# A relative-position attention layer on one core: one bias term computed on the queries' rows and moved by transfers, in place of PE transposes

## The reference

```python
q, k, v = (shape_heads(x @ W + b) for W, b in ...)      # 16 batches, 16 heads, 256 tokens, 8 features
scores = einsum('bhsd,bhkd->bhsk', q, k) / sqrt(24)
c2p = einsum('bhsd,hkd->bhsk', q, pos_k)                # 64 buckets
c2p = take_along_axis(c2p, idx(s - k))                  # -> [s, k], value depends on bucket(s - k)
p2c = take_along_axis(einsum('bhsd,hkd->bhsk', k, pos_q), idx(k - s)).swapaxes(-1, -2)
probs = softmax(scores + (c2p + p2c) / 4)
ctx = einsum('bhsk,bhkd->bhsd', probs, v)
```

## Time and profile before

| | |
|---|---|
| median of 3 runs | 1324.26 us (1322.44 to 1327.71) |
| the profiled execution, its own time | 1330.51 us |
| its span in the trace | 1328.7 us |
| mean granted TensorE clock | 0.886 of full speed |
| busy: PE, DVE, ACT, POOL | 1048.3, 863.0, 727.5, 460.4 us |

### The profile page before, as it was taken

How to read it: one execution, slowest core, us unless ns; L and a number is a source line. 1 busy time by engine, 2 the same in 40 slices (tenths; PEclk the granted TensorE clock), 3 DMA queues, 4 the chain that set the end, 5 groups by cost and what they waited for, 6 DMA issues and landing times. The chain is left out here.

```text
span 1328.7 us, 34742 instructions
## 1 busy us (share of the span) xinstructions
PE 1048.3 (79%) x9380; PEld 834.1 (63%) x9380; DVE 863.0 (65%) x2997; ACT 727.5 (55%) x1755; POOL 460.4 (35%) x506
## 2 busy tenths in 40 slices
PE   4793515787353899999999999999999998734886
PEld 3793513777232677777777777777777776624776
DVE  6886754555570677777777777777677775652554
ACT  2236411344282677777777777777677774212443
POOL 2503213765200433333333333333333332005764
PEclk9897556999585899999999999999999998656999
DMA  5920052331263222221212222221312220033431
GB/s 136 227 52 0 0 180 92 111 103 54 72 254 120 64 59 62 59 68 50 69 50 69 56 63 67 59 69 50 69 50 69 55 55 1 1 147 97 114 96 42
DMA packets 83508, 103.23 MB, mean 78 GB/s; under 512 B 16473, under 2 KB 71200, under 8 KB 82944
## 3 DMA queue, kind: packets, MB, share of 16 engines
q1 hardware_dynamic: 77824, 89.92, 25.1%
q0 software_dynamic: 5632, 12.70, 2.8%
HBM read 67.86 MB, written 35.74 MB: 78 GB/s over the span
## 5 line engine op out<-in xcount | busy, mean ns | idle before, releaser
L1230 POOL TENSOR_SCALAR ds_scores<-ds_scores,ds_max 128x256 f32<-128x256 f32 x256 | 236.3, 923 | 434.3 <-DVE ds_max L1468 434.2
L1460 DVE TENSOR_TENSOR ds_p2c<-ds_bank,ds_p2c 128x512 f32<-128x512 f32 x256 | 176.4, 689 | 147.9 <-PE ds_bank L1289 113.4
L1468 DVE CUSTOM_DVE_ANT_0 ds_scores<-ds_bank,ds_p2c 128x256 f32<-128x256 f32 x512 | 197.2, 423 | 0.2 <-DVE ds_p2c L1460 0.2
L1289 PE MATMUL ds_bank<-all_constants,ds_c2p_t 128*128 128x128 f32 x1024 | 165.4, 284 | 0.0
L1407 ACT ACTIVATE all_xt<-ds_bank 128x512 f32<-128x512 f32 x256 | 152.6, 596 | 21.4 <-PE ds_bank L1307 8.9
L1307 PE MATMUL ds_bank<-all_constants,ds_scores 128*128 128x128 f32 x1024 | 154.6, 273 | 2.4 <-ACT all_xt L1407 1.6
L1289 PEld LDWEIGHTS ds_bank<-all_constants,ds_c2p_t 128*128 128x128 f32 x1024 | 111.3, 141 | 31.9 <-issue 20.7
L1307 PEld LDWEIGHTS ds_bank<-all_constants,ds_scores 128*128 128x128 f32 x1024 | 120.2, 140 | 7.6 <-issue 2.0
L1390 ACT ACTIVATE ds_c2p_t<-ds_bank 128x256 f32<-128x256 f32 x256 | 77.6, 390 | 56.7 <-PE ds_bank L1280 56.7
L1383 ACT ACTIVATE ds_p2c<-ds_bank 64x512 f32<-64x512 f32 x128 | 75.7, 591 | 54.7 <-PE ds_bank L1261 31.6
L1280 PE MATMUL ds_bank<-d_qr,ds_tab 64*128 64x128 f32 x1024 | 77.3, 292 | 33.1 <-DMA ds_tab<-scratch_tables 27.8
(11 more groups left out here) (285 smaller groups left out, 2011.8 us busy)
## 6 DMA issues: line engine op xcount, KB each, us to landing
ds_tab<-scratch_tables SPq DMA_DIRECT2D x64, 248.0 KB, 3.5
slots_in<-all_zero SPq DMA_DIRECT2D x2, 5180.0 KB, 37.9
ds_qs<-scratch_q_parts SPq DMA_DIRECT2D x32, 288.0 KB
ds_ks<-scratch_k_parts SPq DMA_DIRECT2D x96, 96.0 KB
d_qr<-scratch_qk SPq DMA_DIRECT2D x512, 4.0 KB
d_kr<-scratch_qk SPq DMA_DIRECT2D x512, 4.0 KB
0fe_xb<-slots_in SPq DMA_DIRECT2D x40, 129.5 KB, 2.1
1fe_xb<-slots_in SPq DMA_DIRECT2D x40, 129.5 KB, 2.1
```

The source lines that it names most:

```text
L1230: pool.tensor_scalar(S[b % NS][:, 1, :], S[b % NS][:, 1, :], mx[:, 2 * b + 1:2 * b + 2], None, ALU.subtract).then_inc(s_sub1, 1)
L1289: last = pe.transpose(pt1[b % 2][:, st * SEQ + kt * P:st * SEQ + (kt + 1) * P], CT[half][:, kt, b, st * P:(st + 1) * P], con["ident"])
L1460: dve.tensor_tensor(z, pt1[b % 2][:, :].rearrange("p (a k) -> p a k", a=2), z, ALU.add).then_inc(s_z, 1)
L1468: last = dve.tensor_tensor_reduce(out=S[b % NS][:, st, :], in0=pqk[b % 2][:, st * SEQ:(st + 1) * SEQ], in1=PC[half][:, st, b, :], scale=1. ...
```

## The change

The c2p term is made the other way round. The sparse query rows are the stationary operand and the table moves, so the term comes out with (token group, batch) on partitions and keys along the row. Four matmuls of 64 rows by 64 columns are laid side by side, for two groups of tokens at once. This is one fill "c2p", of which a unit has four (`CROSS`): 8 matmuls with 256 moving columns, into two PSUM banks `pc[0]` and `pc[1]` (those that held the results of `t1`). ACT copies each bank (128x512) into one of four slots of a new tile `STAGE`. From there transfers (`spread`) bring it to the queries' rows of `CT`, which is now laid (query, batch, half, key). For each of the four fills there are three transfers: 64 partitions of 2 KB to 8 partitions of 16 KB, twice, and 128 partitions of 2 KB to 16 partitions of 16 KB. The transposes `t1` go away, and DVE adds `CT` from SBUF. The scores are written back into `PC` rather than into `S`. The "far", "edge", "near" and "pair" fills of c2p go away, and with them the table `far_e`. The two row tiles become one tile `QKR`, filled by 16 transfers of 8 KB rather than 32 of 4 KB. Such a transfer stands on SP's queue in groups of four between the spreads. DVE waits at the start of each unit for all twelve spreads of that unit.

```diff
@@ attend
-        ENDS = [m.sb(f"ends{i}", [9 * DB, 2, 2 * FAR], BF16) for i in range(2)]
-        CT = [m.sb(f"c2p_t{i}", [P, 2, HALF, SEQ]) for i in range(2)]
+        ENDS = [m.sb(f"ends{i}", [9 * DB, 2 * FAR], BF16) for i in range(2)]
+        CT = [m.sb(f"c2p{i}", [P, HALF, 2, SEQ]) for i in range(2)]
+        STAGE = m.sb("stage", [P, 4, 2 * SEQ])
-        S = [m.sb(f"scores{i}", [P, 2, SEQ]) for i in range(NS)]
-        pb, pt1, pqk, pt2, pav = bank[0:2], bank[2:4], bank[4:6], bank[6], bank[7]
+        pb, pc, pqk, pt2, pav = bank[0:2], bank[2:4], bank[4:6], bank[6], bank[7]
+        CROSS = [("c2p", 0, i) for i in range(NB16 // 4)]
-        FILLS = [PAIRS[0][0], PAIRS[0][1], PAIRS[1][0], FARS[0][0], EDGE[0], FARS[0][1], NEAR[0],
-                 PAIRS[1][1], FARS[1][0], NEAR[1], FARS[1][1], EDGE[1]]
+        FILLS = [CROSS[0], CROSS[1], NEAR, CROSS[2], FARS[0], PAIRS[0], CROSS[3], PAIRS[1], FARS[1], EDGE]
-        SHARE = [1, 1, 1, 2, 2, 1, 2, 2]
+        SHARE = [1, 1, 1, 1, 2, 1, 2, 1]
@@ SP
+            def load_rows(head, half, first, count):
+                for s in range(first, first + count):
+                    at = slice(s * P, (s + 1) * P)
+                    sp.dma_start(QKR[half][(15 - s) * DB:(16 - s) * DB, :, at],
+                                 dram["qk"][:, bass.ds(head * DB, DB), half * HT + at.start:half * HT + at.stop].rearrange("j p n -> p j n")).then_inc(s_rows[half], 16)
+            def spread(head, half, i):
+                u = 2 * head + half
+                sp.wait_ge(s_cc, CC * u + 2 * i + 1)
+                sp.sem_inc(s_go_sp, 1)
+                for r in range(2):
+                    at = 16 * (2 * i) + 8 * (1 - r)
+                    sp.dma_start(CT[half][at:at + 8, :, :, :].rearrange("p b t k -> p (b t k)"), STAGE[64 * r:64 * (r + 1), 2 * (i % 2), :]).then_inc(s_ct[i % 2], 16)
+                sp.wait_ge(s_cc, CC * u + 2 * i + 2)
+                sp.sem_inc(s_go_sp, 1)
+                at = 16 * (2 * i + 1)
+                sp.dma_start(CT[half][at:at + 16, :, :, :].rearrange("p b t k -> p (b t k)"), STAGE[:, 2 * (i % 2) + 1, :]).then_inc(s_ct[i % 2], 16)
@@ SP, heads
-                        load_rows(head + 1, half)
+                        sp.wait_ge(s_cm, CM * (u + 1))
+                        sp.sem_inc(s_go_sp, 1)
+                        load_tables(head + 1, half)
+                    for i in range(len(CROSS)):
+                        if not last:
+                            load_rows(head + 1, half, 4 * i, 4)
+                        if not (last and half == 1):
+                            spread(*following(head, half), i)
@@ PE, fill
+                if what == "c2p":
+                    if where > 0 or not (isinstance(u, int) and u == 0):
+                        pe.wait_ge(s_cc, CC * u + 2 * where)
+                    for st in range(2):
+                        for swap in range(2):
+                            g = 8 * st + 2 * where + swap
+                            c = TABLE - SEQ - 16 * g
+                            for tile in range(2):
+                                rows, to = slice(tile * 64, (tile + 1) * 64), tile ^ swap
+                                own = QKR[half][rows, 0, :].rearrange("p (m g) -> p g m", g=NB16)[:, g, 64 * (1 - tile):64 * (2 - tile)]
+                                last = pe.matmul(pc[swap][to * 64:(to + 1) * 64, st * SEQ:(st + 1) * SEQ], own, TAB[half][rows, 0, c:c + SEQ],
+                                                 start=True, stop=True)
...
@@ ACT, copy
+                if what == "c2p":
+                    if where > 1 or not (isinstance(u, int) and u == 0):
+                        act.wait_ge(s_ct[where % 2], CD * u + 48 * (where // 2))
+                    for swap in range(2):
+                        act.wait_ge(s_cm, CM * u + 4 * where + 4)
+                        act.activation(STAGE[:, 2 * (where % 2) + swap, :], pc[swap][:, :], ACT.Copy).then_inc(s_cc, 1)
+                    return
@@ DVE
-                dve.wait_ge(s_t1, step + 1)
-                dve.tensor_tensor(z, pt1[b % 2][:, :].rearrange("p (a k) -> p a k", a=2), z, ALU.add).then_inc(s_z, 1)
+                dve.tensor_tensor(z, CT[half][:, b, :, :], z, ALU.add).then_inc(s_z, 1)
@@ DVE, heads
+                    for s_copied in s_ct:
+                        dve.wait_ge(s_copied, CD * (u + 1))
```

More of the change, by code:

```diff
@@ L839, in disentangled_attention_layer @@
         bo = m.sb("bo", [P, D])
-        QR, KR = ([m.sb(f"{n}{i}", [P, TOKENS // 2]) for i in range(2)] for n in ("qr", "kr"))
+        QKR = [m.sb(f"qkr{i}", [P, 2, TOKENS // 2]) for i in range(2)]
         with ExitStack() as inner:
@@ L1003, in stored @@
     def stored(self, sp):
[L1004 removed]
+        sp.wait_ge(self.s_out, 16 * 4)
     def scalar(self, act):
@@ L1257, in fill @@
                 if what == "edge":
-                    pe.wait_ge(s_stack[half], 16 * 6 * (head + 1))
+                    pe.wait_ge(s_stack[half], 16 * 5 * (head + 1))
                     for side, grp, _ in INNER:
                         own = slice(side * 64, (side + 1) * 64)
-                        last = pe.matmul(pb[FIRST[n] % 2][own, :], ENDS[half][:, kind, side * FAR + own.start:side * FAR + own.stop],
-                                         (QS, KS)[kind][half][:, :].rearrange("p (b s) -> p b s", b=HALF)[:, :, grp * 16:grp * 16 + 64],
+                        last = pe.matmul(pb[FIRST[n] % 2][own, :], ENDS[half][:, side * FAR + own.start:side * FAR + own.stop],
+                                         KS[half][:, :].rearrange("p (b s) -> p b s", b=HALF)[:, :, grp * 16:grp * 16 + 64],
                                          start=True, stop=True)
@@ L1283, in fill @@
                             last.then_inc(s_bm, 1)
-            def t1(step, half, b):
-                pe.wait_ge(s_z, step + 1)
-                for st in range(2):
-                    for kt in range(2):
-                        last = pe.transpose(pt1[b % 2][:, st * SEQ + kt * P:st * SEQ + (kt + 1) * P],
-                                            CT[half][:, kt, b, st * P:(st + 1) * P], con["ident"])
-                last.then_inc(s_t1, 1)
             def qk(step, half, b):
@@ L1341, in heads @@
                             av(*before)
+                        if n % 4 == 0 and (before := group_before(head, half, n, 8)):
+                            back(*before)
                         if not (last and half == 1):
@@ L1345, in heads @@
                                 done += 1
-                        if n % 4 == 0 and (before := group_before(head, half, n, 8)):
-                            back(*before)
             pe.sem_inc(s_t2, NS)
@@ L1439, in copy @@
                 what, kind, where = FILLS[n]
-                if what == "far" and kind == 1:
+                if what == "far":
                     side, quad = where
                     dve.wait_ge(s_bm, (2 * head + half) * BM + FIRST[n] + 1)
-                    dve.tensor_copy((CT, PC)[kind][half][:, side, :, quad * 64:(quad + 1) * 64],
+                    dve.tensor_copy(PC[half][:, side, :, quad * 64:(quad + 1) * 64],
                                     pb[FIRST[n] % 2][:, :].rearrange("p (b s) -> p b s", b=HALF)).then_inc(s_bd, 1)
```

108 lines of the change are left out of this document (52 added, 56 removed).

## The result

The changed kernel takes 1692.2 us (1688.8 to 1695.7), the kernel before 1326.0 on the same chip: a ratio of 1.2765, 95% interval 1.2721 to 1.2809, some 366 us slower. The forecast was 1756, within 1400 to 1930.

The account below looks back on a forecast made before the run. Attention looked bound by PE, with SP's issuing close behind; afterwards by the lower DMA engines at 35.1 us a unit. 31 periods of 13.65 us more (+423) and +9 at the start gave 1756 us, within 1400 to 1930.

Parts of the forecast that it names:

- PE and ACT: Work in one attention unit after the change: PE 16.2 us with four parts side by side (20.5 if two), ACT 14.8.
- the worst case of 22.6: DVE's unit: 15.2 us becomes at most 22.6 if the new addition waits for POOL, at most 7.4 us.
- The path: The lower DMA engines decide a unit, 35.1 us; PE, ACT, DVE and POOL are covered, and SP has room.
- The price of the spreads: Transfers to few partitions cost 7.0 GB/s for each partition written, from `KS`: 56 GB/s for 8, 112 for 16.
- The sum of 35.1: Lower DMA engines' time in one unit: 28.1 us of spreads and 7.0 of other transfers, not hidden below that.
- The term of 28.1 for the spreads: Three transfers of 2.34 us each add to 7.02 us a fill, 28.1 us for a unit's four fills.
- the 7.0 forecast: What the lower DMA engines carry besides spreads in a unit: `QS` and `KS` 2.8 us, tables 1.7, rows 2.3, `ENDS` 0.2.
- Half of it overlaps: Rival: a fill's two 8-partition transfers run at once, a unit takes 25.7 us, +139, 1463 us; chance 0.10.
- I add no gaps: SP's queue stays filled despite two fills' `STAGE` slots: 7 us of DMA work against about 3 for copy, issue and landing.
- the 18 us expected at DVE's first addition: Sign in the profile: DVE's first addition of each unit waits some 18 us a unit for DMA `ds_c2p`.
- The start: First addition of attention moves from 438.87 us to about 448, as the first unit's fills take 28.1: +9 us.
- The rival on the other side: Rival: the destination doesn't matter, DMA engines need 14.5 us a unit, a period of 19 gives 1254 us; chance 0.12.

Follow-up runs that it names:

- l_nospread_order: Kernel without spreads or waits for them, c2p term left out, with another order of fills and of SP's queue: ratio 0.9706 to the kernel before, period 19.8 us.
- p_order: Changed kernel, spreads as they are, with another order of the fills and of SP's queue alone: ratio 1.277 to the kernel before, period 32.6 us.
- a_stride: Changed kernel with the same spreads written to partitions four apart, so the term lands on wrong rows: ratio 1.1181 to the kernel before, period 26.4 us.
- b_nospread: Changed kernel with no spreads and no waits for them, CT set to zero once: ratio 1.0344 to the kernel before, period 22.6 us.
- d_swap: Changed kernel with ACT swapping the first bank's halves, one 16-partition transfer replacing two of 8: ratio 1.1939 to the kernel before, period 29.7 us.
- k_swap_order: Kernel with ACT's swapped halves and two 16-partition transfers a fill, given another order of fills and of SP's queue: ratio 1.1736 to before, period 28.9 us.
- m_two_queues: Changed kernel with the 16-partition transfers issued by ACT after its copies in place of SP: ratio 1.3471 to the kernel before, period 36.5 us.

## Why the prediction was right, point by point

- **PE and ACT.** Forecast 16.2 us a unit on PE with four parts side by side. At the full clock it is 17.5 (l_nospread_order), the fills 4.6 for 4.3: the parts do run together. ACT: 14.5 for 14.8. DVE: 16.0, between 15.2 and the worst case of 22.6. The new addition was hardly held up, 699 ns for 689; POOL's subtraction went from 923 to 1045 ns and DVE's from 344 to 456. PE was busy 22.8 us of the 32.6, not about half: its granted clock was 0.79 there. It still fits into the period, as forecast. SP: 19.0, within 18.8 to 23.5.
- **The path.** The DMA engines set the period: that holds. Seven or more of the sixteen are busy in 97.5% of the time, at a share of 0.68 and 103 GB/s (forecast: near 0.65 and 97); another order of the fills brings nothing (p_order); and with the partitions written four apart 6.5 us of a unit go away (a_stride).
- **The price of the spreads: the rule was wrong, the rate usable.** 7.0 GB/s for each partition, from `KS`, gave 56 and 112 GB/s; the windows show 49 to 61 with 8 partitions nearly alone and some 115 with 16. Eight partitions four apart take no such time (packets of 110 ns in a_stride, for 231), and 64 neighbours got 197 to 262 GB/s where 128 partitions got 426. The unit is a group of neighbouring partitions, 24 to 31 GB/s for each four (49 to 61 / 2, 115 / 4, `KS` 168 / 6), and 64 partitions have only 8 such ways (25 to 33 each). This is what the Trainium skill says (SBUF — State Buffer, "Door 1: The DMA port swizzle"): four neighbours share a port, partitions 32 further on use the same ones, and a range of 64 covers eight of the sixteen. The trace agrees, within that spread, for 8, 16, 24 and 64 partitions. For 8, 16 and 24 neighbours a price per partition and one per group come to the same, so the wrong rule gave a usable rate.
- **The sum of 35.1: near, and in part by luck.** The period was 32.9; the 2.2 us over 31 units are 68 us, and the forecast was 64 too high. The term of 28.1 for the spreads is the mis-sized one: their packets lasted 231 ns in the mean, not 293. Of the 1024 a unit, 768 are on the lower engines as the prediction counts them, 96 for each. If those last as long as the mean, they take 22.2 us (an estimate); even if the other 256 took only 84 ns, about the shortest there are, it is under 27. The rest was dearer beside the spreads than alone. A table packet lasts 157 ns, and 116 in b_nospread; one of `QS` or `KS` 361, and 238. In the mean of all sixteen engines the rest takes 22.4 - 1024 x 0.231 / 16 = 7.6 us a unit, and 0.21 x 22.6 = 4.7 without spreads. How much of it lies on the lower engines is not known; by the estimate above up to 10.7, for the 7.0 forecast, and then the two errors offset each other. In any case fixed prices don't add up here, since packets last longer beside slow writes: for d_swap the same kind of sum gave 23.5 us and missed by 6.2.
- **"Half of it overlaps".** It did not end there (25.7 us). But the half-share windows carry 71 GB/s in the mean, above the 56 of one 8-partition transfer. That the engines of one transfer don't keep step, so that some already write the next one's partitions, is argued, not shown.
- **"I add no gaps" and where the stall shows.** Right in the sum: the engines hardly pause and the order changed nothing (p_order). Wrong in the place: of the 18 us expected at DVE's first addition, 5.4 are there, and another 5.2 come to DVE through ACT's wait for a `STAGE` slot and PE's for ACT. The rest of its idle time stands before other results of PE.
- **The start.** +9 forecast, 8.0 measured.
- **The rival on the other side.** It promised 1254 us if destinations cost nothing. That floor was wrong too: a sum of busy times is not a period. b_nospread, with no spreads at all, has 22.6, above the 21.45 of before; only another order brings 19.8. That is near the 19 put down for SP, but SP issues no spreads there, so the nearness shows nothing.

## What to carry to other kernels

Price a transfer into SBUF by the groups of neighbouring partitions that it writes, not by its bytes alone, and expect the transfers beside it to slow down too: here moving the data twice, out to DRAM and back to all 128 partitions, was 8.8 us a unit cheaper than once to 8 and 16 neighbours. Before work is taken off the fullest engine, look at what the others then wait for: with the spreads left out entirely the change was still slower, until its fills were put in another order. And read a stall back through the in-order queues; a wait of ACT for a buffer appeared as PE's and DVE's.

## What the hardware showed that was not expected

- A read of 1 MB to 64 neighbouring partitions runs at 197 to 262 GB/s in 1 us windows (25 to 33 for each of eight ways), one of the same size to all 128 at 426.
- Slow writes lengthen the packets of other transfers: one of the tables, to 128 partitions, lasts 116 ns in b_nospread, 157 in the changed kernel and 206 in k_swap_order.
- The share of the DMA engines is no measure of their work: for the same bytes 22.3 us a unit in d_swap and 26.0 in k_swap_order, which only issues them earlier and closer together.
- Two queues at once (m_two_queues) moved 88 GB/s at a share of 0.65, one queue 103 at 0.68.
- PE's granted clock was 1.00 in this stretch before and in l_nospread_order, 0.81 in the changed kernel, where PE waits a third of the time.
